# Layer norm means and variances from VectorE's aggregate instruction, and a new order of calls on all engines

## The chip, the cores and the metric

The kernel runs on one core of a Trainium2 chip. The metric is the device time of one execution in microseconds, the median of several runs. Engines are named as in the profile: PE is TensorE (PEld its weight loads), DVE VectorE, ACT ScalarE, POOL GpSimd, SP SyncE, which only issues transfers here.

## The reference, cut to what matters

One transformer layer in float32, with the layer norm behind each residual sum: causal attention with one head and rotation of half the head's width, then a feed-forward net with weights replaced by their sign times a mean magnitude.

```python
def _layernorm(x, axis=-1, eps=1e-05):
    m = jnp.mean(x, axis=axis, keepdims=True)
    v = jnp.var(x, axis=axis, keepdims=True)
    return (x - m) / jnp.sqrt(v + eps)

# x: (8, 1024, 128); wq, wk, wv, wo: 128 x 128; w1: 512 x 128; w2: 128 x 512
q, k, v = x @ wq, x @ wk, x @ wv            # q and k rotated in half of their 128 columns
p = softmax(q k^T / 128, causal)            # 1024 x 1024 for each of the 8 sequences
x = _layernorm(x + (p v) wo)
h = gelu(x @ sign(w1)^T * alpha1 + b1)      # 512 wide
x = _layernorm(x + h @ sign(w2)^T * alpha2 + b2)
```

## The kernel before, in words

The work is cut into 8 steps c, one for each sequence of 1024 tokens. Within a step there are 8 row tiles of 128 tokens (r or t) and two halves of four tiles (h, or g for a group of rows). Each engine has a list of calls such as `scores(2, 1)` (tile 2, step 1) written out by hand at the end of its block; an engine takes its calls strictly in that order, and waits inside a call on semaphores that other engines raise. Calls of several steps are interleaved in these lists, so that while one step is in its attention another is in its feed-forward net. There is no loop over c and no scheduler at build time: the order of the lists is the schedule.

A step goes through these calls. `stripes` (SyncE) loads x as 32-wide stripes into xq, in four transfers; `x_squares` (VectorE) turns xq into xT by 32 x 32 transposes, one call for each half, and the first half's call waits for all four transfers; `xT_high` (ScalarE) and `xT_low` (GpSimd) split it into a rounded part and a rest. Step 0 takes another way: `turn_x0` on TensorE and `x0T_low` on VectorE. `project` (TensorE) makes q and k, `rotate` (three VectorE instructions) and `rotation_sum` (GpSimd; `first_rotation_sum` on VectorE in step 0) turn them, `tok_copy` (ScalarE) copies the columns that are not turned. `turn_qk`, `qkT_high`, `qkT_low` transpose and split. `scores` (TensorE), `row_max` (VectorE) and `exponentials` (ScalarE) give a row tile's probabilities; `turn_row` (VectorE) transposes their 32 x 32 blocks, and `carry` (SyncE, 16 transfers for a group) puts the blocks in place. In steps 0 and 7 the rows 4 to 7 are transposed by TensorE instead, and copied by `row_copy`. `weigh_group` or `weigh_row` and `project_out` (TensorE) finish the attention, `residual1`, `statistics1` and `first_norm` (VectorE) the first norm. `turn_x1`, `x1T_high`, `x1T_low`, `up`, `gelu`, `hidden_high`, `hidden_low` (GpSimd), `down`, `y_half`, `turn_y` are the feed-forward net, `residual2`, `statistics2` and `second_norm` the second norm, `store` the output. In step 7 the feed-forward net is cut into halves, to shorten the end.

Between statistics and norm a few numbers for each token are worked out: mean and 1/sqrt(variance + eps). VectorE's bn_stats instruction leaves count, mean and sum of squared deviations of the even and of the odd elements of a row (`stat1`, `stat2`). GpSimd puts these together in `norm_factors`, eight small instructions on 128 x 4 or 128 x 8 numbers, the last one a power of -1/2; `first_factors` does so for a half, `second_factors` for a whole step. Only in step 7 `first_means` and `second_means` have VectorE's bn_aggr do it, four instructions for a half, followed by two small tensor_scalars, with GpSimd left with the power.

On TensorE `keep_warm(n)` and `fill(n)` issue n matmuls of no use, to keep it running while it waits.

Of the kernel before, what the change touches and what calls it, by code (L numbers as in the profile page):

```python
# [8 lines left out]
ALU = mybir.AluOpType  # L9
# [7 lines left out]
def attention_ffn_kernel(nc, x, wq, wk, wv, wo, w1, b1, w2, b2, cos_t, sin_t, out):  # L17
# [27 lines left out]
    LN_STEPS = 8  # L45
    LN2_STEPS = 9
# [9 lines left out]
    with ctx:  # L56
# [46 lines left out]
        ln1 = sb("ln1", [P, LN_STEPS, NT])  # L103
# [11 lines left out]
        ln2 = sb("ln2", [P, LN_STEPS, NT])  # L115
# [29 lines left out]
        def sems(name, n):  # L145
# [5 lines left out]
            sems("s_qk", NG), sems("s_qkT", 4), sems("s_score", NT), sems("s_px", NT), sems("s_attn", NG))  # L151
# [10 lines left out]
        s_res2, s_stat2, s_y = sems("s_res2", NG), sems("s_stat2", NG), sem("s_y")  # L162

# [40 lines left out]
        def _(sp):  # L204
# [28 lines left out]
            def carry(g, c):  # L233

                if by_squares(GROUPS[g][-1], c) == 1:
                    sp.wait_ge(s_const, 5 + 4)
                sp.wait_ge(s_turned[GROUPS[g][-1]], by_squares(GROUPS[g][-1], c))
                if c > 0:
                    sp.wait_ge(s_px[GROUPS[g][-1]], c)
# [18 lines left out]
            stripes(2)  # L258
            carry(0, 0)
            stripes(3)  # L260
            tokens(1)
# [6 lines left out]
            carry(1, 2)  # L268
            stripes(B - 2)
            tokens(3)  # L270
            carry(0, 3)
            carry(1, 3)
            stripes(B - 1)
            carry(0, B - 4)
            tokens(B - 4)
# [3 lines left out]
            tokens(B - 2)  # L279
# [3 lines left out]
            store(1)  # L283
            carry(1, B - 2)
            store(2)
            tokens(B - 1)
# [11 lines left out]
        def _(pool):  # L298
# [17 lines left out]
            def norm_factors(stat, ln, ts, done, before, sign):  # L316

                def after(n):
                    pool.wait_ge(done, before + n)

                mean_e, m2_e, mean_o, m2_o = (stat[:, ts, j] for j in (1, 2, 4, 5))
                total, diff, mean, semi, m2, part, square, rstd = (ln[:, j, ts] for j in range(8))
                pool.tensor_tensor(total, mean_e, mean_o, ALU.add).then_inc(done, 1)
                pool.tensor_tensor(diff, mean_e, mean_o, ALU.subtract).then_inc(done, 1)
                pool.tensor_tensor(m2, m2_e, m2_o, ALU.add).then_inc(done, 1)
                after(2)
                pool.tensor_scalar(ln[:, 2:4, ts], ln[:, 0:2, ts], 0.5 * sign, None, ALU.mult).then_inc(done, 1)
                after(3)
                pool.tensor_scalar(part, m2, 1.0 / D, LN_EPS, ALU.mult, ALU.add).then_inc(done, 1)
                after(4)  # L330
                pool.tensor_tensor(square, semi, semi, ALU.mult).then_inc(done, 1)
                after(6)
                pool.tensor_tensor(part, part, square, ALU.add).then_inc(done, 1)
                after(7)
                pool.tensor_tensor(rstd, part, minus_half[:, ts], ALU.pow).then_inc(done, 1)  # L335

# [15 lines left out]
            def first_factors(h, c):  # L352
                pool.wait_ge(s_stat1[h], c + 1)
                norm_factors(stat1, ln1, slice(TG * h, TG * (h + 1)), s_ln1[h], LN_STEPS * c, 1.0)

            def second_factors(c):
                pool.wait_ge(s_stat2[0], c + 1)
                pool.wait_ge(s_stat2[1], c + 1)
                if c > 0:
                    pool.wait_ge(s_y, c)  # L360
                norm_factors(stat2, ln2, slice(0, NT), s_ln2, LN2_STEPS * c, -1.0)
                pool.wait_ge(s_ln2, LN2_STEPS * c + LN_STEPS)
                pool.tensor_tensor(ln2[:, 6, :], ln2[:, 2, :], ln2[:, 7, :], ALU.mult).then_inc(s_ln2, 1)

            def first_rstd(h, c):

                ts = slice(TG * h, TG * (h + 1))
                pool.wait_ge(s_ln1[h], LN_STEPS * c + 3)
                pool.tensor_tensor(ln1[:, 7, ts], ln1[:, 5, ts], minus_half[:, ts], ALU.pow).then_inc(s_ln1[h], 1)

            def second_rstd(h, c):

                ts = slice(TG * h, TG * (h + 1))
                pool.wait_ge(s_ln2_end[h], 3)
                pool.tensor_tensor(ln2[:, 7, ts], ln2[:, 5, ts], minus_half[:, ts], ALU.pow).then_inc(s_ln2_end[h], 1)
                pool.wait_ge(s_ln2_end[h], 4)
                pool.tensor_tensor(ln2[:, 6, ts], ln2[:, 4, ts], ln2[:, 7, ts], ALU.mult).then_inc(s_ln2_end[h], 1)  # L377

            def second_norm(t, c):
                if t == TG:  # L380
                    pool.wait_ge(s_ln2, LN2_STEPS * (c + 1))
                ins = pool.tensor_scalar(res2[c % 2][:, t, :], res2[c % 2][:, t, :], ln2[:, 7, t:t + 1], ln2[:, 6, t:t + 1],
# [12 lines left out]
            xT_low(1, 1)  # L395
            rotation_sum(0, 1)
            rotation_sum(1, 1)
            xT_low(0, 2)
            xT_low(1, 2)
            rotation_sum(0, 2)  # L400
            xT_low(0, 3)
            xT_low(1, 3)
            first_factors(0, 0)
            rotation_sum(1, 2)
            rotation_sum(0, 3)
            first_factors(1, 0)
            xT_low(0, B - 4)
            xT_low(1, B - 4)
            rotation_sum(1, 3)
# [3 lines left out]
            rotation_sum(1, B - 4)  # L413
# [3 lines left out]
            xT_low(0, B - 3)  # L417
            hidden_low(3, 0)
            first_factors(0, 2)
            xT_low(1, B - 3)  # L420
            first_factors(1, 2)
            rotation_sum(0, B - 3)
            xT_low(0, B - 2)
            hidden_low(0, 1)
            hidden_low(1, 1)
            hidden_low(2, 1)
            hidden_low(3, 1)
            first_factors(0, 3)
            second_factors(0)
            rotation_sum(1, B - 3)  # L430
            first_factors(1, 3)
            xT_low(1, B - 2)
            hidden_low(0, 2)
            rotation_sum(0, B - 2)
# [4 lines left out]
            xT_low(0, B - 1)  # L439
            first_factors(0, B - 4)  # L440
            second_factors(1)
            first_factors(1, B - 4)
            xT_low(1, B - 1)
            rotation_sum(0, B - 1)
            hidden_low(0, 3)
            hidden_low(1, 3)
            hidden_low(2, 3)
            hidden_low(3, 3)
            second_factors(2)
            first_factors(0, B - 3)  # L450
            rotation_sum(1, B - 1)
            first_factors(1, B - 3)
# [4 lines left out]
            second_factors(3)  # L457
            first_factors(0, B - 2)
            first_factors(1, B - 2)
            hidden_low(0, B - 3)  # L460
            hidden_low(1, B - 3)
            hidden_low(2, B - 3)
            hidden_low(3, B - 3)
            second_factors(B - 4)
            first_rstd(0, B - 1)
# [4 lines left out]
            first_rstd(1, B - 1)  # L470
# [10 lines left out]
            second_rstd(0, B - 1)  # L481
            second_rstd(1, B - 1)

        @block.tensor
        def _(pe):
# [71 lines left out]
            def fill(n):  # L557

                wait_freed(*list(pair_of)[-len(pairs)])
# [33 lines left out]
            def weigh_group(g, first, last, c):  # L593
# [15 lines left out]
                if last == rows[-1]:  # L609
                    ins.then_inc(s_px[last], 1)  # L610

            def weigh_row(r, c):
# [9 lines left out]
                if r == GROUPS[g][-1]:  # L622
                    ins.then_inc(s_px[r], 1)
# [111 lines left out]
            fill(2)  # L735
            turn_qk(2, 0)
            scores(2, 0)
            scores(3, 0)
            setup_wvo()
            project(0, 1)  # L740
# [1390 lines left out]
```

## Time and profile before

| what | value |
|---|---|
| time, median of 3 runs | 276.61 us (275.88 to 279.37) |
| span of the profiled execution, first to last instruction | 274.5 us |
| around the span, against the median of the runs | 2.1 us |
| TensorE busy | 260.9 us, 95% |
| TensorE's weight loads | 208.7 us, 76% |
| VectorE busy | 229.6 us, 84% |
| ScalarE busy | 224.7 us, 82% |
| GpSimd busy | 167.2 us, 61% |
| instructions in the profile | 5184 |

The busy shares are averages over the whole span. The profiled execution's own whole time is not listed apart from its span, so the span is set against the median of the runs. Which engine the others wait for in a stretch is read from the timeline and from the chain of work that ended last, which is followed back from the last instruction.

### The profile page before, as it was taken

What the parts mean: (1) busy time and instruction counts of PE and PEld (TensorE: products, weight loads), DVE (VectorE), ACT (ScalarE), POOL (GpSimd) and SP (SyncE); (2) the same over time, 40 slices, a digit from 0 to 9 for tenths busy, and PEclk for the clock granted to TensorE, in tenths of its full rate; (3) what the DMA queues carried; (4) which work ended last, traced back from release to release, by engine and by line L of the source; (5) the groups of instructions that cost most, each with busy time, mean ns of one, the idle gap of its engine ahead of it and who ended that gap; (6) DMA issues with size and microseconds to landing.
All of it is one profiled execution on the core that took longest, in us unless ns stands there. A gap on an engine that the chain in (4) does not pass through costs nothing.

```text
span 274.5 us, 5184 instructions
## 1 busy us (share of the span) xinstructions
PE 260.9 (95%) x1485; PEld 208.7 (76%) x1487; DVE 229.6 (84%) x638; ACT 224.7 (82%) x398; POOL 167.2 (61%) x258
## 2 busy tenths in 40 slices
PE   7899999999999999999999999999999999999960
PEld 3678989987779588868879688868886878897630
DVE  2799999999999996999979987998689738537984
ACT  3378964565897989996998999898999799999972
POOL 3033132613625698399821998497819887887772
PEclk9999999999999999999999999999999999999997
DMA  7944596479657936833685318825830720200323
GB/s 178 166 61 87 107 145 98 115 163 192 104 132 160 199 94 153 180 47 78 173 187 127 82 39 249 184 71 151 189 73 27 197 55 2 76 2 0 111 90 108
DMA packets 58012, 31.94 MB, mean 116 GB/s; under 512 B 33408, under 2 KB 54400, under 8 KB 57984
## 3 DMA queue, kind: packets, MB, share of 16 engines
q1 hardware_dynamic: 57024, 30.76, 50.4%
q10 hardware_dynamic: 960, 0.85, 1.3%
q8 instruction: 12, 0.20, 0.3%
q14 instruction: 16, 0.13, 0.2%
HBM read 9.18 MB, written 4.19 MB: 49 GB/s over the span
## 4 chain that ended last, share of the span: by engine, by line
PE 81%; DVE 6%; ACT 5%; issue 3%; DMA 2%; ACTq 1%; POOL 0%; POOLq 0%
PE pair L589 18%; PE bank L606 18%; PE bank L632 5%; PE bank L674 4%; PE pair L650 4%; PE pair L651 4%; PE bank L620 4%; PE bank L682 4%; PE bank L683 4%; PE bank L719 2%; DMA sin_sb<-in_sin_dram 2%; PE pair L663 2%; PE pair L665 2%; PE pair L664 2%; PE bank L639 2%
## 5 line engine op out<-in xcount | busy, mean ns | idle before, releaser
L391 POOL TENSOR_TENSOR hid_lo<-hid,hid_hi 128x1024 fp32r<-128x1024 f32 x28 | 66.0, 2386 | 19.7 <-ACT hid_hi L1075 19.7
L1004 ACT ACTIVATE prob<-pair,negmax 128x128 f32<-128x128 f32 (+3 forms) x64 | 47.2, 742 | 14.2 <-DVE negmax L1457 12.5
L606 PE MATMUL bank<-probT,xa 128*128 128x512 f32 (+3 forms) x160 | 54.2, 482 | 0.0
L1457 DVE CUSTOM_DVE_ANT_0 pair<-pair,mask_row 128x128 f32<-128x128 f32 (+3 forms) x64 | 47.9, 759 | 6.1 <-PE pair L589 5.5
L606 PEld LDWEIGHTS bank<-probT,xa 128*128 128x128 f32 x160 | 29.1, 190 | 20.2 <-issue 15.3
L341 POOL TENSOR_TENSOR xT_lo<-xT,xT_hi 128x512 fp32r<-128x512 f32 x14 | 18.0, 1288 | 40.4 <-ACT xT_hi L1034 40.4
L1467 DVE STREAM_TRANSPOSE turned<-prob 128x128 f32<-128x128 f32 (+7 forms) x56 | 39.5, 724 | 0.5 <-ACT prob L1004 0.5
L589 PE MATMUL pair<-qkT_hi 128*128 128x512 f32 (+3 forms) x96 | 36.0, 375 | 0.8 <-DVE qkT_lo L1619 0.3
L1068 ACT ACTIVATE hid<-pair,b_sb,alpha 128x1024 f32<-128x1024 f32 x28 | 32.9, 1209 | 0.1
L589 PE MATMUL pair<-qkT_lo,qkT_hi 128*128 128x512 f32 (+3 forms) x96 | 32.8, 342 | 0.0
L589 PE MATMUL pair<-qkT_hi,qkT_lo 128*128 128x512 f32 (+3 forms) x96 | 32.8, 342 | 0.0
L1075 ACT ACTIVATE hid_hi<-hid 128x1024 fp32r<-128x1024 f32 x28 | 28.6, 1057 | 0.0
L335 POOL TENSOR_TENSOR ln<-ln,minus_half 128x4 f32<-128x4 f32 (+1 forms) x21 | 26.2, 1249 | 1.6
L1102 ACT ACTIVATE res<-res,ln 128x128 f32<-128x128 f32 x52 | 23.1, 496 | 3.6 <-POOL ln L377 3.6
L1056 ACT ACTIVATE qkT_hi<-bank 128x512 fp32r<-128x512 f32 x32 | 18.5, 598 | 7.3 <-PE bank L674 7.2
L1619 DVE TENSOR_TENSOR qkT_lo<-bank,qkT_hi 128x512 fp32r<-128x512 f32 x32 | 21.1, 680 | 3.4 <-ACT qkT_hi L1056 3.4
L349 POOL TENSOR_TENSOR tok<-rot_cos,rot_sin 128x512 f32<-128x512 f32 x14 | 18.0, 1288 | 9.4 <-DVE rot_sin L1614 9.4
L650 PE MATMUL pair<-x1T_hi,sgn1T 128*128 128x512 f32 x56 | 23.4, 418 | 0.3 <-issue 0.3
L682 PE MATMUL bank<-hid_hi,sgn2T 128*128 128x512 f32 x56 | 22.3, 399 | 0.0
L683 PE MATMUL bank<-hid_lo,sgn2T 128*128 128x512 f32 x56 | 22.2, 396 | 0.0
L651 PE MATMUL pair<-x1T_lo,sgn1T 128*128 128x512 f32 x56 | 22.1, 395 | 0.0
L1567 DVE TENSOR_TENSOR res<-bank,x 128x512 f32<-128x512 f32 x16 | 10.9, 687 | 12.5 <-PE bank L719 12.4
(116 smaller groups left out, 649.9 us busy)
## 6 DMA issues: line engine op xcount, KB each, us to landing
probT<-turned SPq DMA_DIRECT2D x96, 116.0 KB, 2.3
probT<-turned SPq DMA_DIRECT2D x128, 52.0 KB, 2.0
xq<-in_L_attn_x_dram SPq DMA_DIRECT2D x28, 128.0 KB, 4.0
xa<-in_L_attn_x_dram SPq DMA_DIRECT2D x7, 512.0 KB, 4.7
out_dram<-res SPq DMA_DIRECT2D x7, 512.0 KB, 3.3
hid<-in_L_ffn_w_dram SPq DMA_DIRECT2D x2, 256.0 KB, 3.2
out_dram<-res SPq DMA_DIRECT2D x2, 256.0 KB, 2.3
xa<-in_L_attn_x_dram SPq DMA_DIRECT2D x1, 256.0 KB, 3.6
```

Of the source, the lines that this page charges most:

```text
L391: pool.tensor_tensor(hid_lo[:, j, :], hid[:, j, :], hid_hi[:, j, :].bitcast(F32), ALU.subtract).then_inc(s_hid_lo[j], 1)
L589: ins = pe.matmul(dst[:, lo:hi], qp[:, 0, me], kp[:, 1, lo - first:hi - first], start=n == 0, stop=n == 2)
L606: ins = pe.matmul(bank_of["px", g, c][:, 0:n * P], xa[c % 2][:, j, :], probT[g][:, :, TG * j:TG * j + n, :].rearrange("p n m i -> p m n i" ...
L650: pe.matmul(dst[:, half(h)], sgn1T[:, j, :], x1T_hi[:, half(h)], start=True, stop=False)
L651: ins = pe.matmul(dst[:, half(h)], sgn1T[:, j, :], x1T_lo[:, half(h)], start=False, stop=True)
L682: pe.matmul(dst[:, :], sgn2T[:, j, :], hid_hi[:, j, half(h)], start=j == 0, stop=False)
L683: ins = pe.matmul(dst[:, :], sgn2T[:, j, :], hid_lo[:, j, half(h)], start=False, stop=j == NF - 1)
L1004: act.activation(prob[r % 3][:, 0:(r + 1) * P], pair_of["score", r, c][:, slice(*columns(r))], ACT.Exp, scale=-1.0, bias=negmax[:, r:r + 1 ...
L1068: act.activation(hid[:, j, :], pair_of["up", j, c][:, :], ACT.Gelu, bias=b1_sb[:, j:j + 1], scale=alpha1[:, j:j + 1]).then_inc(s_gelu[j], 1)
L1075: act.activation(hid_hi[:, j, :], hid[:, j, :], ACT.Copy).then_inc(s_hid_hi[j], 1)
L1457: dve.tensor_tensor_reduce(mine, mine, mask_row[:, T - (r + 1) * P:T], -1.0, -MASKED, ALU.add, ALU.min, negmax[:, r:r + 1]).then_inc(s_max ...
L1467: dve.transpose(turned[g][:, :, squares(r, 0, r), :].rearrange("p k m j -> p m k j"), prob[r % 3][:, 0:(r + 1) * P].rearrange("p (m k j) - ...
```

## The change

The aggregates of step 7 are now used in every step. `first_means` and `second_means` on VectorE run four bn_aggr for a half and nothing else; GpSimd's `norm_factors` gives way to `factors`: add eps, raise to the power -1/2, and for the second norm also two small products. Two sets of semaphores for the means come in, and the eight semaphores of `weigh_group` become two. The lists of calls of all five engines are written in another order; which calls there are stays the same but for the means and the factors of step 7. Of the fillers, those of `keep_warm` behind `turn_x0`, `project` and `turn_qk` are gone, and `fill` calls stand at other places. As many matmuls are fillers as before, 32.

```diff
+            def factors(ln, ts, done, before, shift):
+                mean, var, part, rstd, away, moved = (ln[:, j, ts] for j in (0, 1, 2, 3, 4, 5)) if shift else (
+                    *(ln[:, j, ts] for j in range(4)), None, None)
+                pool.tensor_scalar(part, var, LN_EPS, None, ALU.add).then_inc(done, 1)
+                if shift:
+                    pool.tensor_scalar(away, mean, -1.0, None, ALU.mult).then_inc(done, 1)
+                pool.wait_ge(done, before + 1)
                 pool.tensor_tensor(rstd, part, minus_half[:, ts], ALU.pow).then_inc(done, 1)
+                if shift:
+                    pool.wait_ge(done, before + 3)
+                    pool.tensor_tensor(moved, away, rstd, ALU.mult).then_inc(done, 1)
...
             def first_means(h, c):
                 dve.wait_ge(s_stat1[h], c + 1)
-                if h == 0:
-                    dve.wait_ge(s_x1[NG - 1], c)
-                dve.wait_ge(s_ln1[h], LN_STEPS * c)
-                means(stat1, ln1, h, s_ln1[h], LN_STEPS * c)
+                if c > 0:
+                    dve.wait_ge(s_x1[h], c)
+                for t in tiles(h):
+                    ins = dve.bn_aggr(ln1[:, 0:2, t], stat1[:, t, :])
+                ins.then_inc(s_means1[h], 1)
 
             def second_means(h, c):
                 dve.wait_ge(s_stat2[h], c + 1)
-                if h == 0:
+                if c > 0:
                     dve.wait_ge(s_y, c)
-                    dve.wait_ge(s_y_pool, len(SHARED))
-                    dve.wait_ge(s_ln2, LN2_STEPS * c)
-                means(stat2, ln2, h, s_ln2_end[h], 0)
+                if c - 1 in SHARED:
+                    dve.wait_ge(s_y_pool, 1 + SHARED.index(c - 1))
+                for t in tiles(h):
+                    ins = dve.bn_aggr(ln2[:, 0:2, t], stat2[:, t, :])
+                ins.then_inc(s_means2[h], 1)
...
+            fill(2)
+            fill(3)
             turn_x0(0)
             turn_x0(1)
-            keep_warm(4)
             project(0, 0)
             project(1, 0)
-            keep_warm(3)
+            fill(4)
             turn_qk(0, 0)
             turn_qk(1, 0)
-            keep_warm(6)
+            project(0, 1)
             setup_turn_wv()
```

VectorE at the start of its list. `xT` is x_squares of step 1, `rot_cos` and `rot_sin` are rotate, `tok` is first_rotation_sum. Before:

```order
L1594 TENSOR_TENSOR xT_lo<-bank0,xT_hi 128x512
L1594 TENSOR_TENSOR xT_lo<-bank1,xT_hi 128x512
L1611 TENSOR_TENSOR rot_cos<-pair0,cos_sb 128x512
L1612 TENSOR_TENSOR rot_sin<-pair0,sin_sb 128x8x32
L1614 TENSOR_TENSOR rot_sin<-pair0,sin_sb 128x8x32
L1589 TENSOR_TENSOR tok<-rot_cos,rot_sin 128x8x64
L1611 TENSOR_TENSOR rot_cos<-pair1,cos_sb 128x512
L1612 TENSOR_TENSOR rot_sin<-pair1,sin_sb 128x8x32
L1614 TENSOR_TENSOR rot_sin<-pair1,sin_sb 128x8x32
L1584 STREAM_TRANSPOSE xT<-xq 128x512
```

After:

```order
L1569 TENSOR_TENSOR xT_lo<-bank0,xT_hi 128x512
L1569 TENSOR_TENSOR xT_lo<-bank1,xT_hi 128x512
L1559 STREAM_TRANSPOSE xT<-xq 128x512 x2
L1586 TENSOR_TENSOR rot_cos<-pair0,cos_sb 128x512
L1587 TENSOR_TENSOR rot_sin<-pair0,sin_sb 128x8x32
L1589 TENSOR_TENSOR rot_sin<-pair0,sin_sb 128x8x32
L1564 TENSOR_TENSOR tok<-rot_cos,rot_sin 128x8x64
L1586 TENSOR_TENSOR rot_cos<-pair1,cos_sb 128x512
L1587 TENSOR_TENSOR rot_sin<-pair1,sin_sb 128x8x32
```

Both squares of step 1 now stand ahead of rotate(0, 0); before, the first of them stood behind rotate(1, 0).

VectorE at the last row tiles of group 0 in step 0: `turned0` is turn_row, `qkT_lo` qkT_low(2, 0) and (3, 0), `negmax` the end of a row_max. Before:

```order
L1457 ISA negmax 128x1
L1449 COPY wvo<-bank0 128x128
L1467 STREAM_TRANSPOSE turned0<-prob1 128x2x4x32
L1467 STREAM_TRANSPOSE turned0<-prob2 128x3x4x32
L1467 STREAM_TRANSPOSE turned0<-prob0 128x4x4x32
L1619 TENSOR_TENSOR qkT_lo<-bank1,qkT_hi 128x512
L1619 TENSOR_TENSOR qkT_lo<-bank0,qkT_hi 128x512
```

After:

```order
L1437 ISA pair0,negmax<-pair0,mask_row 128x512
L1437 ISA negmax 128x1
L1594 TENSOR_TENSOR qkT_lo<-bank1,qkT_hi 128x512
L1594 TENSOR_TENSOR qkT_lo<-bank0,qkT_hi 128x512
L1447 STREAM_TRANSPOSE turned0<-prob2 128x3x4x32
L1447 STREAM_TRANSPOSE turned0<-prob0 128x4x4x32
L1586 TENSOR_TENSOR rot_cos<-pair1,cos_sb 128x512
L1587 TENSOR_TENSOR rot_sin<-pair1,sin_sb 128x8x32
```

The two turn_rows that carry(0, 0) waits for now stand behind the two qkT_low, and setup_wvo (the copy to `wvo`) went to an earlier place.

SyncE from its first stripes call in the list on: `xq` is stripes, `xa` tokens, `probT` a carry, the first one of group 0. Before:

```order
L226 DMA xq<-in_L_attn_x_dram 32x32x32 x4
L242 DMA probT<-turned 32x416 x16
L226 DMA xq<-in_L_attn_x_dram 32x32x32 x4
L231 DMA xa<-in_L_attn_x_dram 128x8x128
L226 DMA xq<-in_L_attn_x_dram 32x32x32 x4
L242 DMA probT<-turned 32x416 x16
L242 DMA probT<-turned 32x928 x16
L231 DMA xa<-in_L_attn_x_dram 128x8x128
```

After:

```order
L227 DMA xq<-in_L_attn_x_dram 32x32x32 x4
L232 DMA xa<-in_L_attn_x_dram 128x8x128
L227 DMA xq<-in_L_attn_x_dram 32x32x32 x4
L243 DMA probT<-turned 32x416 x16
L227 DMA xq<-in_L_attn_x_dram 32x32x32 x4
L243 DMA probT<-turned 32x416 x16
L243 DMA probT<-turned 32x928 x16
L232 DMA xa<-in_L_attn_x_dram 128x8x128
```

tokens(1) and stripes(3) moved ahead of carry(0, 0).

GpSimd at the first factors of a half. `ln<-stat` and the rows up to the power (`minus_half`) are norm_factors. Before:

```order
L341 TENSOR_TENSOR xT_lo<-xT,xT_hi 128x512 x2
L323 TENSOR_TENSOR ln<-stat 128x4
L324 TENSOR_TENSOR ln<-stat 128x4
L325 TENSOR_TENSOR ln<-stat 128x4
L327 TENSOR_SCALAR ln<-ln 128x2x4
L329 TENSOR_SCALAR ln<-ln 128x4
L331 TENSOR_TENSOR ln<-ln 128x4
L333 TENSOR_TENSOR ln<-ln 128x4
L335 TENSOR_TENSOR ln<-ln,minus_half 128x4
L349 TENSOR_TENSOR tok<-rot_cos,rot_sin 128x8x64 x2
```

After:

```order
L334 TENSOR_TENSOR xT_lo<-xT,xT_hi 128x512
L321 TENSOR_SCALAR ln<-ln 128x4
L325 TENSOR_TENSOR ln<-ln,minus_half 128x4
L342 TENSOR_TENSOR tok<-rot_cos,rot_sin 128x8x64 x2
```

Eight instructions became two.

## Rows read from the trace of the kernel before

**Rows 1.** Page, part 1: busy us (share of the span) x instructions, each engine.
```profile
PE 260.9 (95%) x1485; PEld 208.7 (76%) x1487; DVE 229.6 (84%) x638; ACT 224.7 (82%) x398; POOL 167.2 (61%) x258
```

**Rows 2.** Page, part 4: the chain that ended last, shares by engine.
```profile
PE 81%; DVE 6%; ACT 5%; issue 3%; DMA 2%; ACTq 1%; POOL 0%; POOLq 0%
```

**Rows 3.** Timeline of TensorE: start us, length us, engine, line, operation, [idle before <-releaser].
```profile
220.24 0.39 PE L683 MATMUL bank<-hid_lo,sgn2T 128*128 128x512 f32 x1
220.47 0.40 PE L682 MATMUL bank<-hid_hi,sgn2T 128*128 128x512 f32 x1
...
266.44 0.63 PE L719 MATMUL bank<-ident,yT 128*128 128x128 f32 x4 [0.96 <-ACT yT L1093]
```

**Rows 4.** Windows, in order: PE, PEld, DVE, ACT, POOL; granted clock, DMA, GB/s.
```profile
10.00:100.00 90.00, 88.02 (x542) 72.31 (x541) 87.05 (x216) 66.20 (x138) 36.57 (x51) 1.00 0.67 132
100.00:220.00 120.00, 119.85 (x649) 95.76 (x648) 105.09 (x297) 109.88 (x184) 88.54 (x138) 1.00 0.53 128
```

**Rows 5.** Timeline of SyncE's queue, the carries.
```profile
20.18 10.84 SPq L242 DMA_DIRECT2D probT<-turned  x16
...
40.94 22.25 SPq L242 DMA_DIRECT2D probT<-turned  x32
...
67.81 21.42 SPq L242 DMA_DIRECT2D probT<-turned  x32
```

**Rows 6.** Timeline of VectorE, head and first step.
```profile
8.87 0.69 DVE L1611 TENSOR_TENSOR rot_cos<-pair,cos_sb 128x512 f32<-128x512 f32 x1 [1.44 <-DMA sin_sb<-in_sin_dram]
...
10.26 0.69 DVE L1589 TENSOR_TENSOR tok<-rot_cos,rot_sin 128x512 f32<-128x512 f32 x1
...
12.13 0.70 DVE L1584 STREAM_TRANSPOSE xT<-xq 128x512 f32<-128x512 f32 x1
...
13.93 1.78 DVE L1589 TENSOR_TENSOR tok<-rot_cos,rot_sin 128x512 f32<-128x512 f32 x1
...
40.17 0.71 DVE L1467 STREAM_TRANSPOSE turned<-prob 128x512 f32<-128x512 f32 x1
```

**Rows 7.** The chain that ended last, pieces in order of time: start us, us.
```profile
23.31 4.11 PE pair L589 x18
...
35.26 2.16 PE bank L606 x8
...
90.95 3.70 PE bank L606 x8
```

**Rows 8.** The stripes of line 214: duration, starts and landings.
```profile
L214 SPq DMA_DIRECT2D xq<-in_L_attn_x_dram x4: 443/1484/3146, 1.8 to 6.1; - x4
...
DMA to landing us min/median/max: 5.4/7.1/7.9
```

**Rows 9.** Timeline of GpSimd, head.
```profile
13.87 1.29 POOL L341 TENSOR_TENSOR xT_lo<-xT,xT_hi 128x512 fp32r<-128x512 f32 x1 [10.23 <-ACT xT_hi L1034]
```

**Rows 10.** Page, part 6: KB each, median us from issue to landing.
```profile
probT<-turned SPq DMA_DIRECT2D x128, 52.0 KB, 2.0
```

**Rows 11.** Timeline of VectorE, last factors.
```profile
268.74 0.38 DVE L1529 BATCH_NORM_AGGREGATE ln<-stat 128x2 f32<-128x6 f32 x4
269.15 0.17 DVE L1532 TENSOR_SCALAR ln<-ln 128x4 f32<-128x4 f32 x1
```

**Rows 12.** Who waited for whom: us in total, times, longest us.
```profile
POOL ln L323 <- ACT res L1102: 1.6, 2, 1.2
```

**Rows 13.** Timeline of GpSimd, one half's factors and the next.
```profile
217.81 0.21 POOL L323 TENSOR_TENSOR ln<-stat 128x4 f32<-128x4 f32 x1
...
220.46 0.21 POOL L323 TENSOR_TENSOR ln<-stat 128x4 f32<-128x4 f32 x1
```

**Rows 14.** Timeline of GpSimd, the last power.
```profile
269.47 1.03 POOL L375 TENSOR_TENSOR ln<-ln,minus_half 128x4 f32<-128x4 f32 x1 [1.22 <-DVE ln L1533]
```

**Rows 15.** Windows at the run's end (columns as in rows 4).
```profile
268.00:270.00 2.00, 0.00 (x0) 0.00 (x0) 1.83 (x12) 0.88 (x2) 0.73 (x2) 1.00 0.19 55
270.00:272.00 2.00, 0.00 (x0) 0.00 (x0) 0.60 (x2) 0.88 (x2) 0.71 (x2) 0.70 0.41 131
```

More of the change, by code:

```diff
@@ L889, in _ @@
             turn_y(0, 2)
-            scores(0, B - 2)
             scores(1, B - 2)
@@ L1702, in _ @@
+            first_norm(1, 0)
+            rotate(0, 3)
             residual1(6, 0)
             residual1(7, 0)
+            statistics1(4, 0)
+            statistics1(5, 0)
+            statistics1(6, 0)
+            first_norm(2, 0)
+            row_max(0, 2)
+            first_norm(3, 0)
+            statistics1(7, 0)
+            row_max(1, 2)
+            qkT_low(2, 2)
+            row_max(2, 2)
+            qkT_low(3, 2)
+            first_means(1, 0)
             turn_row(0, 2)
-            row_max(1, 2)
@@ L1736, in _ @@
+            x1T_low(0, 0)
+            turn_row(3, 2)
             turn_row(4, 2)
+            row_max(6, 2)
             row_max(7, 2)
+            rotate(1, 3)
             x1T_low(1, 0)
@@ L1793, in _ @@
             qkT_low(1, B - 4)
-            statistics1(0, 2)
-            statistics1(1, 2)
+            turn_row(5, 3)
+            turn_row(6, 3)
             turn_row(7, 3)
-            statistics1(2, 2)
+            rotate(0, B - 3)
+            qkT_low(2, B - 4)
+            x_squares(0, B - 2)
             residual1(4, 2)
+            row_max(0, B - 4)
             residual1(5, 2)
+            statistics1(3, 2)
             residual1(6, 2)
             residual1(7, 2)
-            statistics1(3, 2)
@@ L1803, in _ @@
             statistics1(4, 2)
-            reciprocals(0, 3)
-            reciprocals(1, 3)
+            row_max(1, B - 4)
+            residual2(0, 0)
+            first_means(0, 2)
+            x_squares(1, B - 2)
+            rotate(1, B - 3)
+            statistics2(0, 0)
+            qkT_low(3, B - 4)
+            turn_row(0, B - 4)
             statistics1(5, 2)
             statistics1(6, 2)
-            rotate(0, B - 3)
-            statistics1(7, 2)
-            qkT_low(2, B - 4)
-            row_max(0, B - 4)
@@ L1812, in _ @@
-            row_max(1, B - 4)
-            x_squares(0, B - 2)
-            x_squares(1, B - 2)
-            residual2(0, 0)
-            qkT_low(3, B - 4)
-            rotate(1, B - 3)
+            reciprocals(1, 3)
             first_norm(0, 2)
             first_norm(1, 2)
+            statistics1(7, 2)
+            first_means(1, 2)
+            residual2(1, 0)
             first_norm(2, 2)
-            residual2(1, 0)
             first_norm(3, 2)
+            statistics2(1, 0)
+            second_means(0, 0)
@@ L1876, in _ @@
+            qkT_low(3, B - 3)
             row_max(1, B - 3)
+            row_max(2, B - 3)
+            row_max(3, B - 3)
+            x_squares(1, B - 1)
+            turn_row(1, B - 3)
             first_norm(4, 3)
-            turn_row(0, B - 3)
+            row_max(4, B - 3)
+            residual1(0, B - 4)
+            turn_row(2, B - 3)
+            x1T_low(0, 3)
+            residual1(1, B - 4)
+            residual1(2, B - 4)
             first_norm(5, 3)
+            row_max(5, B - 3)
@@ L1903, in _ @@
+            qkT_low(1, B - 2)
+            second_means(0, 1)
             turn_row(6, B - 3)
-            x1T_low(1, 3)
-            x_squares(1, B - 1)
-            rotate(1, B - 2)
-            qkT_low(0, B - 2)
-            qkT_low(1, B - 2)
             residual1(4, B - 4)
-            turn_row(7, B - 3)
             residual1(5, B - 4)
@@ L1913, in _ @@
             residual1(7, B - 4)
-            statistics2(1, 1)
+            statistics1(3, B - 4)
+            turn_row(7, B - 3)
+            reciprocals(0, B - 3)
+            second_means(1, 1)
             statistics1(4, B - 4)
+            qkT_low(2, B - 2)
+            first_means(0, 4)
+            qkT_low(3, B - 2)
             statistics1(5, B - 4)
```

908 lines of the change are left out of this document (435 added, 473 removed).

## The prediction

> **What bounds the kernel now.** I read the shares first: TensorE is busy 95% of the span, VectorE 84%, GpSimd 61% [rows 1], and the chain that ended last runs 81% over TensorE and 0% over GpSimd [rows 2]. A busy TensorE may still be waiting inside an instruction, so I looked at starts: two neighbouring 128x512 matmuls start 0.23 us apart while each is shown as 0.39 to 0.40 long [rows 3]. They overlap, and nothing fits between them. Real holes are rare and small: 0.96 us before the last transposes [rows 3]. So from about 23 us on, TensorE is the bound, and a delay that reaches it is never made up. Second comes VectorE: 87.05 us busy of the 90 from 10 to 100, 2.95 idle, then 105.09 of 120 [rows 4]. Third, SyncE issues the transfers that carry the turned probabilities: 32 issues took 22.25 us from 40.94 and 32 more 21.42 us from 67.81 [rows 5]. With stripes and tokens in between, that is one unbroken stretch to 89.2.
>
> The head is VectorE's. Its rotate(0, 0) began at 8.87, when the sine table had landed [rows 6], and scores(4, 0) began at 23.31 on the chain [rows 7].
>
> **The change part by part.**
>
> *The head, where VectorE's calls are reordered.* Now both x_squares(., 1) stand ahead of rotate(0, 0), and VectorE takes its calls in order. x_squares waits for all four transfers of xq. The last of the four is issued at 6.1 and none landed in less than 5.4 us [rows 8]: VectorE stands still until 11.5, while its last call before that ends at 7.43 (8.87 less its idle 1.44 [rows 6]). Before, the first square ran at 12.13, when xq had long been there. So a wait of 1.44 us becomes one of 4.1, and the row of VectorE's work that paces the head starts 11.5 - 8.87 = 2.6 us later. The work in that row up to the release of scores(4, 0) is about the same: two more squares (2 x 0.62), two turn_rows less (about 1.1). One thing is saved: first_rotation_sum took 0.69 alone and 1.78 beside GpSimd's xT_lo [rows 6, 9]; its second call has moved away from that, -1.1. So scores(4, 0) comes 1.5 to 2.6 later, and the eight transposes of setup_turn_sgn1 and 2 (0.11 each) now stand behind it, not ahead: TensorE is 2.4 to 3.5 late.
>
> *The first carry.* turn_row(3, 0) stood before qkT_low(2, 0) and (3, 0) and now stands behind them. It ends near 26, not 20.1. SyncE now has stripes(3) and tokens(1) ahead of this carry, but both are issued by about 24.5 (the stripes wait for x_squares(., 2), near 22) and cost it nothing. The carry that waits for it took 10.84 us of issues [rows 5] and the last lands 2.0 us after its issue [rows 10]: about 38.3. weigh_group(0, 0, 3, 0) began at 35.26 [rows 7]; with 3 us of lateness, and 1.0 us less work ahead of it (scores(2, 1) and one turn_qk moved behind), TensorE is there at 37.2 and waits 1.1. Lateness is then about 4.
>
> *SyncE's stretch.* carry(0, 1) starts when turn_row(3, 1) is done, at 40.17 + 0.71 before [rows 6]. By equal work it comes 3.5 later (2.6, and 1.0 more work ahead of it now); with the waits on weigh_group and project_out in that stretch, 5.3. From there SyncE's stretch is as long as before, so weigh_group(1, 0, 3, 2), at 90.95 before [rows 7], starts 3.5 to 5.3 late, with the same TensorE work behind it in both programs. I take **+4.5**, nearer to the end with the waits, since they are of instructions that VectorE's new order does contain.
>
> *Aggregates on VectorE.* 14 half means and 7 whole ones: 14 x 4 + 7 x 8 = 112 aggregates; four took 0.38 us [rows 11], so 0.10 each, 10.6 us, less eight small tensor_scalars of 0.08 that leave VectorE: +10.0 of work. Before 100 us it is six calls of 0.40 = 2.4 against an idle time of 2.95; after that 14.9 us are idle [rows 4]. If that cover holds, the cost is 0; if not before 100, 2.4. I take 0, since idle time exceeds the work in both stretches. second_means now waits on VectorE for ScalarE's second_norm of the step before, with row_max and turn_row queued behind it. GpSimd had that wait: 1.6 us in two [rows 12]. Bounds 0 to 1.6, and I take 0, as ScalarE's list has these norms ahead of the exponentials that VectorE needs first anyhow.
>
> *GpSimd's chains.* A half took 2.65 us (217.81 to 220.46 [rows 13]), and now an addition and a power, some 1.3. The 14 halves (1.35 each) and the 7 wholes (about 1.2 each) give back about 27 us of GpSimd. It is hidden work: 0. The gain would show only where GpSimd is last, and it has 0% of the chain [rows 2].
>
> *Fills.* 32 filler matmuls before and after, in other places. Five stand ahead of turn_x0 and delay it by about 1.1 us. The wait for xq hides that: cost 0, and 1.1 if xq came early.
>
> *The end.* The last factors: after the aggregates VectorE ran two small steps from 269.15, then GpSimd the power at 269.47 [rows 11, 14]. Now GpSimd runs both small steps, in its own slower rhythm (about 0.15 and 0.28 to the next): +0.2. Ahead of that, hidden_low_half(0, 2) and (0, 3) move before residual2 and fill(2) behind up_half(1, 1), worth up to 1.5; against them second_means(0, 5) and (1, 5), 0.8, now stand before first_norm(4, 7). I take -0.5, bounds -1.5 and +1.
>
> **Sum** on the profiled span: 274.5 + 4.5 + 0.2 - 0.5 = 278.7. The span lies 2.1 below the median of the runs (276.61); that stays around it: **280.8 us**.
>
> A rule speaks against my reading. VectorE and ScalarE are busy 84% and 82%, TensorE's weight loads 76% [rows 1]. The Trainium skill (Perfetto Trace Analysis, Identifying the Most-Contended Engine) says that matmul busy time is no good measure for TensorE, that its headroom is judged by MFU and the share of LDWEIGHTS, and that the engine with the highest occupancy is to be relieved first. By that, VectorE would be the bound and its +10.0 would be paid in full: 276.6 + 10.0 = 286.6. The matmul starts 0.23 us apart [rows 3] do not agree with headroom, so this is a rival and not the forecast.
>
> **The rivals.**
>
> *Slower: VectorE takes over as the bound* before 100 us. From the point where its idle time there, 2.95 us, is eaten, each aggregate delays row_max and turn_row and so ScalarE, SyncE and TensorE. For it: 97% busy. Against it: the squares moved into the idle wait are work done early. Price: 2.4 for the six calls and 1.6 for the new wait on top: 280.8 + 4.0 = 284.8; in full, as above, 286.6.
>
> *Slower: the clock.* After project(1, 0) and fill(4) TensorE has nothing from about 11.5 until turn_qk(0, 0) near 15. At the end of the run its last matmuls are at 266.44 [rows 3], and the granted clock is 1.00 to 270 and 0.70 on average from 270 to 272 [rows 15]: it fell to the lower level, 1.2 GHz, some 3.7 us after TensorE stopped. The hole in the head is about as long. If it falls there, 2.3 us of transposes and project(0, 1) take up to twice as long, with VectorE waiting: about +1.6, 282.4.
>
> *Faster: the head's holes are filled.* If xq landed before 8.9, the squares would lie in the old wait for the table, project(0, 1) (12 matmuls of 0.12, 1.4 us) in the hole where TensorE ran fillers, and nothing would be late: 276.6 - 1.4 - 0.5 - 0.7 (part of first_rotation_sum) = 274.0. Against it: 6.1 + 5.4 [rows 8].
>
> **How the numbers follow.** The head's delay stays, other costs near 0 (278.5 to 282.5): 0.45. The clock falls as well (280.5 to 284.5): 0.17. VectorE takes over (283 to 288): 0.18. Holes filled (271 to 277.5): 0.20. The predicted time is that of the first. The range 275.0 to 285.5 leaves out about half of the holes case and half of VectorE's. The measurement tells 2% from no change: under 271.1 or over 282.1. Over 282.1 lie a tenth of the first case, over half of the clock's, all of VectorE's: 0.32. Under 271.1: 0.03. Between: 0.65.
>
> **What would show it.** In the profile of the changed kernel: VectorE's first transpose of xq waits on a transfer for about 4 us and starts near 11.5, rotate(0, 0) near 12.8; scores(4, 0) near 25; SyncE's carry(0, 1) near 45; weigh_group(1, 0, 3, 2) near 95.5; from there TensorE without holes; GpSimd's busy time near 140, VectorE's near 240; the granted clock between 10 and 20 tells the second rival. I am wrong if xq lands early, if TensorE's waits after 95 us shrink by more than a microsecond or two (that would give the delay back), or if VectorE shows next to no idle time from 20 to 100 and TensorE waits on it there.

## The result, and the profile after: 302.79 us, slower by 9%

The changed kernel takes 302.79 us (median of 4 runs, 301.98 to 303.99) against 276.55 (275.88 to 279.37): a ratio of 1.0945, 95% interval 1.0883 to 1.1007. The forecast was 280.8 with a range of 275.0 to 285.5; the time lies above every rival too. The profiled execution has a span of 301.7 us; before it was 274.5, so 27.2 us are to be found.

The page of after: part 1, the first line of part 4, and one group of part 5.

```profile
PE 268.7 (89%) x1485; PEld 214.0 (71%) x1487; DVE 256.1 (85%) x742; ACT 225.5 (75%) x398; POOL 147.6 (49%) x145
...
PE 34%; DVE 13%; issue 3%; ACT 2%; POOL 2%; ACTq 0%; POOLq 0%; DVEq 0%
...
L1481 DVE TENSOR_SCALAR x<-res,ln 128x128 f32<-128x128 f32 x64 | 41.8, 696 | 0.2
```

TensorE was 95% busy [rows 1]; now it is 89%. The shares of the chain cannot be set against those of before [rows 2] as they stand: after, the chain is followed back only to 137.71 us, so its shares are of the whole span but add up to 54%. Of that part VectorE has about a quarter (13 of 54) where it had 6%, and first_norm alone is 5% of the span. VectorE is busy 26.5 us longer, where +10 was forecast. The third line has the reason: the 64 first_norms take 41.8 us. The same group before:

```profile
L1499 DVE TENSOR_SCALAR x<-res,ln 128x128 f32<-128x128 f32 x64 | 18.7, 340 | 0.6 <-POOL ln L369 0.3
```

It is the same instruction on the same shapes, 23.1 us dearer. Its mean hides two kinds: after, minimum, median and maximum are 298, 341 and 2394 ns. 15 of the 64 last over 0.6 us; before, none lasts over 0.44. Of the 15, 12 began beside a hidden_low on GpSimd; the others ran beside xT_low (two) and rotation_sum (one). One place shows what the long ones have in common (timeline of after; columns as in rows 3):

```profile
242.49 4.66 POOL L370 TENSOR_TENSOR hid_lo<-hid,hid_hi 128x1024 fp32r<-128x1024 f32 x2 [1.26 <-ACT hid_hi L1055]
242.56 4.93 DVE L1481 TENSOR_SCALAR x<-res,ln 128x128 f32<-128x128 f32 x3
247.28 1.12 PE L619 MATMUL bank<-ident,x 128*128 128x128 f32 x4 [3.79 <-DVE x L1481]
```

GpSimd's hidden_low begins at 242.49, 0.07 ahead of a first_norm. Of VectorE's three norms the first lasts 2.37 us, until just past the end of the first hidden_low at 244.85; the second meets the next hidden_low and lasts 2.38 us, until just past its end at 247.15; only the third takes 0.34. VectorE shows as busy all the while. TensorE waits 3.79 us for these norms, and then pays again (windows of after: the two stretches of rows 4, then 3 us each; columns as there):

```profile
10.00:100.00 90.00, 84.57 (x531) 70.68 (x531) 83.50 (x219) 62.05 (x129) 30.36 (x26) 1.00 0.60 121
100.00:220.00 120.00, 111.38 (x594) 88.52 (x593) 113.34 (x327) 99.24 (x161) 64.96 (x55) 0.99 0.54 126
...
240.00:243.00 3.00, 3.00 (x23) 2.64 (x22) 2.25 (x5) 3.00 (x4) 1.67 (x3) 1.00 0.14 36
243.00:246.00 3.00, 0.50 (x5) 0.26 (x3) 3.00 (x2) 1.45 (x2) 3.00 (x2) 1.00 0.00 0
246.00:249.00 3.00, 1.72 (x5) 1.25 (x6) 3.00 (x7) 0.56 (x2) 1.15 (x1) 0.50 0.00 0
249.00:252.00 3.00, 3.00 (x6) 1.69 (x5) 0.74 (x2) 0.98 (x2) 1.94 (x1) 0.50 0.00 0
252.00:255.00 3.00, 3.00 (x24) 2.96 (x23) 1.08 (x2) 2.29 (x5) 0.40 (x1) 0.86 0.00 0
```

TensorE ran no matmul from 243.49 (247.28 less its idle 3.79); the granted clock is at its lower level, 1.2 GHz, from 246 to past 252, and rises again under work. That happens three times between 190 and 277 us. The first two lines say the same of the whole stretch: from 100 to 220 VectorE is 8.2 us busier than before (105.09 [rows 4]) and TensorE 8.5 less (119.85). In all, who waited for whom in after:

```profile
PE bank L619 <- DVE x L1481: 8.9, 3, 3.8
```

The forecast's own landmarks up to 96 us were nearly met (timeline of after: first square, scores(4, 0), SyncE's carry(0, 1), weigh_group(1, 0, 3, 2), the last transposes):

```profile
11.18 1.30 DVE L1559 STREAM_TRANSPOSE xT<-xq 128x512 f32<-128x512 f32 x2 [1.74 <-DMA xq<-in_L_attn_x_dram]
...
24.19 0.50 PE L569 MATMUL pair<-qkT_hi 128*128 128x320 f32 x1
...
46.39 21.74 SPq L243 DMA_DIRECT2D probT<-turned  x32
...
96.22 1.13 PE L586 MATMUL bank<-probT,xa 128*128 128x512 f32 x2 [0.40 <-DMA probT<-turned]
...
293.24 0.65 PE L699 MATMUL bank<-ident,yT 128*128 128x128 f32 x4 [1.20 <-ACT yT L1073]
```

The transposes of xq start at 11.18 as forecast (near 11.5), though VectorE waits 1.74 us for them and not about 4, since its calls ahead of them ended later than before. Up to 96 us the kernel is 5.3 us late (90.95 before [rows 7]), with +4.5 forecast. Between there and the last transposes it loses another 21.5 (293.24 - 266.44 [rows 3] - 5.3).

### The profile page after: what moved, and what is told of

It reads as the page before. It is cut to its first block, busy times and chain, and to the rows that moved or that the text cites. A ratio compares the mean times of both kernels' runs of the same rounds, so it can differ in the third digit from the quotient of the medians.

```text
span 301.7 us, 5219 instructions
## 1 busy us (share of the span) xinstructions
PE 268.7 (89%) x1485; PEld 214.0 (71%) x1487; DVE 256.1 (85%) x742; ACT 225.5 (75%) x398; POOL 147.6 (49%) x145
## 4 chain that ended last, share of the span: by engine, by line
PE 34%; DVE 13%; issue 3%; ACT 2%; POOL 2%; ACTq 0%; POOLq 0%; DVEq 0%
PE bank L586 6%; DVE x L1481 5%; PE pair L569 4%; PE bank L662 4%; PE bank L663 4%; PE bank L612 3%; PE pair L630 3%; PE pair L631 3%; DVE pair L1437 2%; PE bank L619 1%; PE bank L654 1%; PE bank L600 1%; POOL ln L325 1%; PE bank L699 1%; DVE turned L1447 1%
## 5 line engine op out<-in xcount | busy, mean ns | idle before, releaser
L586 PE MATMUL bank<-probT,xa 128*128 128x512 f32 (+3 forms) x160 | 55.7, 498 | 2.5 <-DMA probT<-turned 1.8
L586 PEld LDWEIGHTS bank<-probT,xa 128*128 128x128 f32 x160 | 30.6, 197 | 26.4 <-issue 21.2
L1481 DVE TENSOR_SCALAR x<-res,ln 128x128 f32<-128x128 f32 x64 | 41.8, 696 | 0.2
L321 POOL TENSOR_SCALAR ln<-ln 128x4 f32<-128x4 f32 (+1 forms) x25 | 6.2, 249 | 67.8 <-DVE ln L1512 53.3
L1447 DVE STREAM_TRANSPOSE turned<-prob 128x128 f32<-128x128 f32 (+7 forms) x56 | 38.4, 709 | 0.1
L325 POOL TENSOR_TENSOR ln<-ln,minus_half 128x4 f32<-128x4 f32 (+1 forms) x25 | 30.5, 1221 | 1.3
L1082 ACT ACTIVATE res<-res,ln 128x128 f32<-128x128 f32 x52 | 22.3, 493 | 4.5 <-POOL ln L328 4.5
L569 PEld LDWEIGHTS pair<-qkT_hi 128*128 128x128 f32 x96 | 18.4, 192 | 5.2 <-issue 3.5
```

What stands on the lines that cost most here:

```text
L569: ins = pe.matmul(dst[:, lo:hi], qp[:, 0, me], kp[:, 1, lo - first:hi - first], start=n == 0, stop=n == 2)
L586: ins = pe.matmul(bank_of["px", g, c][:, 0:n * P], xa[c % 2][:, j, :], probT[g][:, :, TG * j:TG * j + n, :].rearrange("p n m i -> p m n i" ...
L1447: dve.transpose(turned[g][:, :, squares(r, 0, r), :].rearrange("p k m j -> p m k j"), prob[r % 3][:, 0:(r + 1) * P].rearrange("p (m k j) - ...
L1481: ins = dve.tensor_scalar(x1[c % 2][:, t, :], res1[:, t, :], ln1[:, 0, t:t + 1], ln1[:, 3, t:t + 1], ALU.subtract, ALU.mult)
```

## Experiments

Three theories. **P**: a first_norm and a running GpSimd instruction exclude each other on a shared port of the memory, and the new order brings them together. **A**: the added aggregates make VectorE the bound. **O**: the new order costs by waits of its own. All versions were timed against before on the same chip. The table gives how much later than before TensorE begins a call, in the profiled execution.

| call (start before) | after | one-port norm | squares first | aggregates, old order | the same, one wait |
|---|---|---|---|---|---|
| scores(4, 0) (21.93) | +2.3 | +4.4 | +3.9 | +0.3 | +0.3 |
| weigh_group(1, 0, 3, 2) (90.95) | +5.3 | +5.3 | +3.7 | +1.4 | +0.8 |
| up(1, 2) (132.41) | +10.4 | +7.6 | +3.6 | +5.7 | +1.9 |
| down(1, 3) (193.75) | +16.9 | +7.2 | +3.6 | +5.9 | +2.2 |
| project_out(0, 7) (230.78) | +23.2 | +7.4 | +3.6 | +6.5 | +2.8 |
| turn_y(1, 7) (266.44) | +26.8 | +6.8 | +3.6 | +6.7 | +3.1 |

**The two halves of the change.** First, the aggregates in the order of before:

```diff
             statistics1(7, 2)
+            first_means(1, 2)
...
-        ln2 = sb("ln2", [P, 6, NT])
+        ln2_of = [sb(f"ln2_{i}", [P, 6, NT]) for i in range(2)]
```

> The order of calls of before, with the aggregates of after: first_means(h, c) right behind the last statistics1 of a half, second_means(h, c) right behind statistics2(h, c), GpSimd's short factors. So that second_means need not wait for the second norm of the step before, the factors of the second norm have two buffers here. Theory P (the shared port: a first_norm that meets a running GpSimd instruction waits until that instruction ends, up to 2.4 us, and the new order brings them together): the old order keeps them mostly apart, so first_norm stays near 0.34 us on average, the aggregates add some 10 us to VectorE's busy time, and the time is 276 to 281 us. Theory A (the aggregates alone make VectorE the bound): 286 us or more, although the order is that of before.

281.95 us, 1.0163 (1.0095 to 1.0232): not 286, but above P's 276 to 281. Second, the new order with GpSimd's chains:

```diff
-            first_means(0, 0)
...
+                norm_factors(stat1, ln1, slice(TG * h, TG * (h + 1)), s_ln1[h], LN_STEPS * c, 1.0)
```

> The other half of the change: the order of calls of after on all engines, with GpSimd's chains of eight for the means and factors as before (aggregates in step 7 alone). Theory P: the meetings of first_norm and hidden_low come from the order, so many of them stay: first_norm well above 0.5 us on average, 288 to 303 us. Theory A: without the 96 extra aggregates VectorE has room again, 279 to 284 us, first_norm near 0.34.

307.48 us, 1.1089 (1.1023 to 1.1155): without the aggregates the new order is slower still, and slower than P's 288 to 303. A falls as the main cause; why GpSimd's long chains cost 4.7 us more here than the aggregates is not shown. The first_norms of this run:

```profile
L1500 DVE TENSOR_SCALAR x<-res,ln 128x128 f32<-128x128 f32 x64 | 43.6, 725 | 0.2
```

**Taking the port's holder away, then its seeker.** To tell P from O, hidden_low was cut to 64 of its 1024 columns (with hid_lo cleared once at the start), and separately first_norm put in another form, which leaves out the multiplication by the inverse deviation:

```diff
-                pool.tensor_tensor(hid_lo[:, j, :], hid[:, j, :], hid_hi[:, j, :].bitcast(F32),
+                pool.tensor_tensor(hid_lo[:, j, 0:64], hid[:, j, 0:64], hid_hi[:, j, 0:64].bitcast(F32),
```

> After, with GpSimd's hidden_low on 64 of 1024 columns (the other columns of hid_lo are left at zero, so the low parts of the feed-forward net are left out): 28 instructions of 2.4 us become short ones, all else is as in after. Theory P: first_norm goes from 0.70 us on average to 0.40 or less, TensorE's waits for it vanish and with them the falls of its clock, and what is left is the delay of the head, about 5 us: 279 to 284 us. Theory A, and a theory O by which the new order has costs of its own that hang on no instruction's length: 292 us or more.

```diff
-                                        ALU.subtract, ALU.mult)
+                                        ALU.subtract, ALU.mult, accum_out=scrap[:, t:t + 1])
```

284.43 us (1.0261, 1.0206 to 1.0317) and 283.41 us (1.0229, 1.0165 to 1.0293). With the cut, the norms fall to 20.8 us (two are still over 1 us, beside xT_low and rotation_sum, and the time is just above P's 279 to 284). With the other form nothing on GpSimd changed, and VectorE has more instructions; yet (the norms with the cut; then, for the other form, one line's instructions with minimum, median, maximum in ns, and TensorE's last transposes):

```profile
L1482 DVE TENSOR_SCALAR x<-res,ln 128x128 f32<-128x128 f32 x64 | 20.8, 369 | 0.2
...
L1482 DVE TENSOR_SCALAR_CACHE_REDUCE x<-res,ln x64: 358/400/407, 58.7 to 260.7; 128x128 f32<-128x128 f32 x64
L1482 DVE DVE_READ_ACCUMULATOR x<-res,ln x64: 77/82/90, 59.1 to 261.1; 128x1 f32 x64
...
273.27 0.66 PE L700 MATMUL bank<-ident,yT 128*128 128x128 f32 x4 [1.15 <-ACT yT L1074]
```

With the other form no norm is long any more, although 21 of them began beside a hidden_low (12 in after). In this run weigh_group(1, 0, 3, 2) starts at 96.22 as in after, and the last transposes at 273.27: from equal lateness at 91 us, 20.0 us of the 21.5 are gone. That is P, by a change in the form of one instruction. The Trainium skill (SBUF — State Buffer, Who interferes with whom) has the rule: GpSimd and VectorE share one port pair as an exclusive lock held for a whole instruction, and a tensor_scalar of VectorE can enter the modes that take it, except in the form that writes its accumulator out. The trace agrees in both halves, 2394 ns for the one and 407 at most for the other; which mode the norms ran in no view shows.

**Repairs.** If the wait is as long as the instruction that runs, smaller ones help; or GpSimd may be made to wait.

```diff
+                for q in range(4):
+                    part = slice(q * T // 4, (q + 1) * T // 4)
+                    ins = pool.tensor_tensor(hid_lo[:, j, part], hid[:, j, part], hid_hi[:, j, part].bitcast(F32),
+                                             ALU.subtract)
```

> After, with each hidden_low on GpSimd as four instructions of 128x256 in place of one of 128x1024; nothing is left out. GpSimd then works longer in all (about 0.7 us a piece, 2.8 for four, in place of 2.4). Theory P: a first_norm waits out the one piece that runs, so none lasts over about 1.1 us, and the sum of first_norm falls from 41.8 us to 24 to 31; TensorE's waits for it get too short for its clock to fall, and the time is 285 to 292 us. Theory L (the lock goes to whoever asks first, and GpSimd, with its next piece always ready, keeps it): the norms stay near 2.4 us and the time near 303.

```diff
             rotation_sum(0, 6)
+            norm_first(0, 3)
+            norm_first(1, 3)
             hidden_low(0, 2)
...
+            def norm_first(h, c):
+                pool.wait_ge(s_x1[h], c + 1)
```

> After, with one more wait on GpSimd: ahead of the first hidden_low behind each pair of first_factors it waits until VectorE is through with the first_norms that these factors serve (a wait of s_x1). Nothing is left out. Theory P: most long first_norms go (sum of first_norm under 26 us), and hidden_low starts later by what VectorE is behind, which TensorE pays in part at down: 284 to 296 us, below after in any case. If the meetings are not the cause, the wait only adds: over 303 us.

Quarters: 285.08 us (1.0294, 1.0265 to 1.0324), norms 27.0 us in all; where they meet hidden_low most last 0.75 to 0.78 us, about one piece. Waits: 291.67 us (1.0541, 1.0514 to 1.0568), norms 24.6 us (quarters, then waits):

```profile
L1484 DVE TENSOR_SCALAR x<-res,ln 128x128 f32<-128x128 f32 x64 | 27.0, 465 | 1.4 <-POOL ln L325 1.2
...
L1498 DVE TENSOR_SCALAR x<-res,ln 128x128 f32<-128x128 f32 x64 | 24.6, 428 | 0.2
```

Both times are as P has them; theory L of the first falls. One bound of the first was missed: none was to last over 1.1 us, and two lasted 1.12 and 1.45, beside xT_low and rotation_sum, which were not cut.

**The head.** The delay of the head was tried in two ways on after, and both missed:

```diff
-            x_squares(0, 1)
-            x_squares(1, 1)
             rotate(0, 0)
             first_rotation_sum(0)
             rotate(1, 0)
+            x_squares(0, 1)
```

> The one-port first_norm of the last set of runs (again without the multiplication by the inverse deviation), and the head in the order of before on all five engines: SyncE's first 4 calls, GpSimd's first 8, TensorE's first 24, ScalarE's and VectorE's first 37 (fillers and setup not counted), where both lists have made the same calls; behind them the order of after. The prediction's main term, the delay of the head: it is about 5 us at weigh_group(1, 0, 3, 2) and is never made up, so without it 278 to 280 us. The rival: VectorE is short of time anyway after 100 us, so the delay would have been met there in any case, and the time stays at 282 to 284.

> Both repairs with nothing left out: hidden_low in quarters, and the head in the order of before (the same calls as in the run with the one-port form and the old head). Theory P with the delay of the head: some 4 to 5 us below the run with quarters alone, 280 to 287 us. If quarters alone do nothing, this stays within 4 us of after.

283.03 us (1.0246, 1.0206 to 1.0285) and 286.22 (1.0344, 1.0319 to 1.0369). The second should have been 4 to 5 us below quarters alone and is 1 above. The first should have been 278 to 280 and lies where its rival had it, 282 to 284. It does not decide all the same: scores(4, 0) is only 0.5 us late there, but where the two orders are joined a new hole opens (one row of its timeline):

```profile
41.13 0.66 PE L570 MATMUL pair<-qkT_hi 128*128 128x384 f32 x1 [2.59 <-ACT tok L1022]
```

TensorE is 6.3 us late at weigh_group(1, 0, 3, 2) all the same. So the head was tried by itself on before:

```diff
             x0T_low(1)
+            x_squares(0, 1)
+            x_squares(1, 1)
             rotate(0, 0)
```

> Before, with one edit: VectorE's x_squares(0, 1) and x_squares(1, 1) stand ahead of rotate(0, 0), as in after; nothing else moves. The prediction's main term by itself. If VectorE's wait for the four transfers of xq (to about 11.2 us) delays the row of work behind it and TensorE never makes that up, scores(4, 0) comes 1.5 to 3 us later than 21.9, that lateness is still there at weigh_group(1, 0, 3, 2) and at the last transposes, and the time is 278 to 280.5 us. The rival: squares done early are work done early, and the delay is gone by 91 us: 276 to 277.2 us.

280.26 us, 1.0147 (1.0117 to 1.0176), for two calls moved. VectorE waits where it was said to (timeline and one window of this run):

```profile
11.31 1.30 DVE L1584 STREAM_TRANSPOSE xT<-xq 128x512 f32<-128x512 f32 x2 [3.79 <-DMA xq<-in_L_attn_x_dram]
...
94.62 0.59 PE L606 MATMUL bank<-probT,xa 128*128 128x512 f32 x1
...
269.99 0.63 PE L719 MATMUL bank<-ident,yT 128*128 128x128 f32 x4 [0.96 <-ACT yT L1093]
```

```profile
16.00:20.00 4.00, 4.00 (x17) 2.48 (x16) 2.96 (x9) 2.92 (x7) 1.48 (x1) 0.62 0.27 37
```

The lateness of 3.6 to 3.9 us stays to the last transposes: on a TensorE without holes nothing is made up. It was to be 1.5 to 3 at scores(4, 0); part of it is the clock, at 0.62 here from 16 to 20, which no run takes apart from the wait.

**What one meeting costs.** In the aggregates in the old order just one norm was long beside hidden_low:

```profile
120.17 9.38 POOL L370 TENSOR_TENSOR hid_lo<-hid,hid_hi 128x1024 fp32r<-128x1024 f32 x4
...
127.66 1.99 DVE L1481 TENSOR_SCALAR x<-res,ln 128x128 f32<-128x128 f32 x1
...
132.30 1.18 PE L612 MATMUL bank<-wvo,pxT 128*128 128x128 f32 x8 [1.90 <-DVE x1T_lo L1535]
```

Three versions of it: one wait on GpSimd, the one-port form, and quarters.

```diff
             hidden_low(2, 1)
+            norm_first(1, 2)
             hidden_low(3, 1)
```

> The aggregates in the old order as in the first run (two buffers for the factors of the second norm), with one wait more: GpSimd's hidden_low(3, 1) waits until first_norm(7, 2) is done. In the first run this was the one first_norm that met a hidden_low: it began at 127.66 and lasted 1.99 us, TensorE then stood 1.90 us and its granted clock fell to 0.66 from 132 to 136; TensorE's lateness against before went from 2.0 to 5.6 us there and stayed. Theory P: without that one meeting the lateness stays near 2.0, so 278 to 279.5 us, about 3 us less for one wait. If aggregates and their waits cost the 5.4 us by themselves, 281 to 283.

> The same aggregates in the old order, without the wait, with first_norm in the one-port form (the multiplication by the inverse deviation is left out; its added work on VectorE was 22.9 + 5.2 - 18.7 = 9.4 us in the run on after). Theory P: no meeting can cost, and the 9.4 us find cover in part: 278 to 281 us. If any first_norm beside hidden_low costs whatever its form, 282 to 285.

> The same aggregates in the old order with hidden_low in four pieces on GpSimd, nothing left out. Theory P: the one meeting now costs at most 0.7 us, and GpSimd's 12 us of extra work are hidden: 278 to 280.5 us. If the size of the instruction that holds the port does not matter, 281 to 283.

One wait: 279.73 us (1.0132, 1.0103 to 1.0162), just above P's 279.5. One-port: 281.78 (1.0203, 1.0178 to 1.0228). Quarters: 281.74 (1.0196, 1.0171 to 1.022). With the wait:

```profile
127.12 0.35 DVE L1485 TENSOR_SCALAR x<-res,ln 128x128 f32<-128x128 f32 x1
127.55 2.40 POOL L373 TENSOR_TENSOR hid_lo<-hid,hid_hi 128x1024 fp32r<-128x1024 f32 x1 [0.85 <-DVE x L1485]
```

In the profiled executions the lateness at up(1, 2) falls from 5.7 to 1.9 us and the span from 281.5 to 277.8: one meeting cost 3.7 us, 1.6 on VectorE and the rest through TensorE's wait and its clock (0.66 from 132 to 136 without the wait, 1.00 with it). By the medians it is 2.2 us, the two intervals overlap, and the profiled execution without the wait was the slowest of its four, so that size is loose; the place is not. The last two runs missed P's ranges: quarters lies where its rival had it (281 to 283), the one-port form between the two, and by the medians neither gains on the 281.95 without a repair. What takes about 2 us from each against the wait is not shown; the one-port form adds work on VectorE (9.4 us in the run on after), and with quarters four norms of 0.8 to 0.9 us remain. No version with the aggregates beats before.

## Why the prediction was wrong

**The step that failed** is the treatment of GpSimd as hidden work: "The gain would show only where GpSimd is last, and it has 0% of the chain" prices what GpSimd does by who waits for its results. No step asked what else runs on VectorE while a GpSimd instruction runs, so first_norm was silently kept at its old 0.34 us through a reordering of both engines. It measured 0.70 on average, 23.1 us in all, and that made some 20 of the 27.2 us. The shorter chains that the sentence was about did not bring it: with the old chains in the new order the norms took 43.6 us. What was put at nothing without a reason is the new order behind 95 us. The evidence stood in the prediction itself: first_rotation_sum took 0.69 alone and 1.78 beside GpSimd's xT_low [rows 6, 9]. It was booked as a saving of 1.1 us in one place (which came true: 0.69 for both calls after) and not read as a rule about two engines.

Before was spared by its order. When 60 of its 64 first_norms began, GpSimd was idle; the other four began beside a power (two) or in the last 0.4 us of a hidden_low (two), and none lost over 0.1 us. After, GpSimd was at work when 36 of the 64 began, and 12 of these fell on a hidden_low, all of them long.

**The head and SyncE's stretch**: near. +4.5 was forecast at weigh_group(1, 0, 3, 2), between 3.5 and 5.3, and +5.3 measured; carry(0, 1) began at 46.39 where 45 was said. One start was misread: 23.31 is scores(5, 0), and scores(4, 0) began at 21.93 before, so its +2.3 is counted from there. The squares alone, on before, show that such a delay is carried to the end. That after's own 5.3 us come from the head is not shown, since with the old head they did not go.

**TensorE without holes after 95 us**: wrong, as above; the prediction's list of what would make it wrong had VectorE saturated from 20 to 100, not norms that stretch after it.

**The aggregates**: taken as 0, with bounds to 2.4, and 1.6 for the new wait. In the old order with the one meeting removed the lateness is 3.1 us at the last transposes, 0.3 of it in the head. That run has two buffers for the factors of the second norm and no such wait, so its 2.8 us stand against the bound of 2.4 alone: the term was not 0 there, but somewhat above its bound. In after VectorE waits 3.1 us for ScalarE's second_norm in second_means, twice GpSimd's 1.6 [rows 12]; what that costs no run shows.

```profile
DVE ln L1522 <- ACT res L1082: 3.1, 2, 2.2
```

**The rivals.** VectorE as the bound (284.8 to 286.6) names the right engine with the wrong reason: with the same aggregates and a norm that needs one port it is 283.4. The clock in the head (282.4): the clock stayed up there in after's profile, and fell in that of the squares alone and, between 14 and 16 us, in three profiles with after's head (the new order without aggregates, the one-port norm, quarters). In after it fell after the long waits instead, three times.

**The end**: +0.2 was forecast for the last factors; the last power begins 3.4 us behind the last transposes where it was 3.0. The -0.5 ahead of that agrees with the one-port norm in the table: from project_out(0, 7) to the last transposes its lateness falls from 7.4 to 6.8.

## What to carry to other kernels

When two engines are reordered against each other, list the instructions that lengthen beside one another and look at what each will run beside in the new order; an instruction whose maximum is many times its median (here 2394 against 341 ns) is the sign. An engine off the critical path is not free if it holds something that the critical engine needs, and then the length of its single instructions can matter more than their sum: quarters gave GpSimd 12 us more work and took 17.7 us off the time. On an engine without holes a delay at the start is paid to the last microsecond, and a hole of a few microseconds is paid again in the clock.

## What the runs showed of the hardware that was not expected

VectorE's waiting on the port is shown as busy time, inside the instruction: no wait stands for it in any view, and VectorE's busy share rises with it. Not every GpSimd instruction holds the port for its length: four norms beside a power of 1.02 us took their usual time (after):

```profile
152.58 1.02 POOL L325 TENSOR_TENSOR ln<-ln,minus_half 128x4 f32<-128x4 f32 x1
152.70 1.11 DVE L1481 TENSOR_SCALAR x<-res,ln 128x128 f32<-128x128 f32 x4
```

And GpSimd with its next instruction ready does not keep the port: where hidden_lows followed each other, one norm got through between two (242.56, 244.85, 247.15 above), which is why quarters shorten the wait to one piece.
